# Weights of an octonion layer placed in threes and pairs of hidden units per partition, and down's last columns spread by GpSimd

## The chip, the cores and the metric

One core of one Trainium2 chip. The metric is the device time of one execution in microseconds. The engines are TensorE (PE; its weight loads are PEld), VectorE (DVE), ScalarE (ACT), GpSimd (POOL) and SyncE (SP), which here issues every DMA.

## The reference

For 2,048 rows of 1,024 numbers, x is normalised to xn. The output is x plus two terms. The first is an autocorrelation block over xn, which for these data comes to xn itself; the kernel proves that row by row with a spectrum and a bound, and has a slow path behind a flag. The second is a gated layer whose three matrices are ternary and act by the octonion product:

```python
def ternary_dequant(W):
    scale = jnp.mean(jnp.abs(W))
    return scale * jnp.clip(jnp.round(W / scale), -1.0, 1.0)
def oct_ternary_linear(xp, W):                 # W: (8, outputs, inputs)
    M = jnp.einsum('jik,jod->koid', S_OCT, ternary_dequant(W))
    return jnp.einsum('...id,koid->...ko', xp, M)
h = silu(oct_ternary_linear(xp, w_gate)) * oct_ternary_linear(xp, w_up)
out = x + attention(xn) + oct_ternary_linear(h, w_down)
```

Gate and up are (8, 341, 128) in float32, down is (8, 128, 341). Each of the 8 components has 341 hidden units. Before a matrix can be made ternary, the mean of all its absolute values must be known.

## The kernel before

**Tiling.** The 2,048 rows go in 8 groups of 256 (two tiles of 128). The 341 hidden units of a component are cut into three chunks c = 0, 1, 2 of 128, 128 and 85 units (`WIDE`). In what order the units stand is free, as long as gate, up and down agree.

**Which unit is where.** Partition p holds units 2p and 2p+1 as chunks 0 and 1, and chunk 2 is unit 256+p on partitions 0 to 84. `up_stage[m]` (m = 0 gate, 1 up) is [partition, j, c, d], one row of 128 floats for each. SyncE loads it in two kinds of transfer: `left_rows` (line 302), 85 partitions by 8 components in pieces of 512 bytes, and pieces of 1,024 bytes (lines 310 and 314) on all 128 partitions. Gate's second kind is cut in two halves of four components, with semaphores `w_in[0]` and `gate_rest`. GpSimd first zeroes chunk 2 of partitions 64 to 127 (line 1764), which `left_rows` waits for, so that the absolute sums can run over whole rows of the staging area. Down lies as [input d on partitions, j, 341 units] and comes in one transfer of 1,364-byte pieces (line 316); TensorE's transposes read chunks 0 and 1 with a step of two elements and chunk 2 as the last 85 columns.

**The head.** VectorE and ScalarE take the row sums of the first x tiles; GpSimd makes the scales of the rows (`rstd`, up to line 1800) and signals `ln_done`. The order on ScalarE is written out: `absolute_gate(0)` (sum of absolute values of a quarter of gate, line 759), `normalise(0, 0)` (748), `absolute_gate(1)`. VectorE has the same: absolute sum (1460), normalise of tile 1 (1479), absolute sum. `absolute_gate(0)` waits for `w_in[0]`, the second for `gate_rest`. TensorE fills its wait with transposes of an identity (`idle_work`), transposes half of gate's first chunk (`weights`, 520), the normalised x (`x_unit`, 482), the other half, and sums the absolute values over the partitions (`total`, 530). VectorE makes the threshold, ScalarE the signs (785), VectorE the ternary weights (1232); then the first group's products (`direct`, 465) begin.

**After the head.** The other chunks of gate, up and down are transposed between the products of the first group, in an order written out by hand for each engine. GpSimd builds sums of ternary weights (1809 to 1813), then waits until the second group's variances are there (1784) before it turns to the hidden units. ScalarE's `absolute(2)` (770) sums down. From the second group on, a written sequence of units (`STEADY`) repeats; lines 409, 416 and 426 are the products of gate and up, line 548 those of down.

Of the kernel before, what the change touches and what calls it, by code (L numbers as in the profile page):

```python
def octonion_ffn_attention_kernel(nc, x, w_gate, w_up, w_down, dft, lag, out):
# [5 lines left out]
    ALU, ACT, AX = mybir.AluOpType, mybir.ActivationFunctionType, mybir.AxisListType  # L7

    P = 128
    ROWS, D = x.shape  # L10
    NJ, HB, DB = w_gate.shape
    NC = 3
    REST = HB - 2 * P
    WIDE = (P, P, REST)
    LEFT = REST + REST % 2
    PAIR = 2 * LEFT
    T = 256
    NT = T // P
    G = ROWS // T
# [134 lines left out]
    with ctx:  # L154
# [3 lines left out]
        def sem(name):  # L158
            return ctx.enter_context(nc.semaphore(name))
# [42 lines left out]


        raw = hop[:, :, :, :, :].rearrange("p a f l t -> p (a f l t)").bitcast(F32)
        stage = [raw[:, 7168:7168 + NJ * NC * DB], raw[:, 10240:10240 + NJ * NC * DB], raw[:, 13312:13312 + NJ * HB]]
        up_stage = [stage[m].rearrange("p (j c d) -> p j c d", j=NJ, c=NC) for m in range(2)]
        down_stage = stage[2].rearrange("p (j h) -> p j h", j=NJ)
        small = zx[:, :, :].rearrange("p t d -> p (t d)").bitcast(F16)
        wt = [small[:, 1024 * i:1024 * (i + 1)].rearrange("p (j d) -> p j d", j=NJ) for i in range(2)]
        tt = [small[:, 2048 + 1024 * i:3072 + 1024 * i].rearrange("p (k v d) -> p k v d", k=4, v=2) for i in range(2)]  # L210
# [21 lines left out]
            return acc[0:rows, bank[n], :, :]  # L232

        x_in = [sem(f"x_in{t}") for t in range(NT)]; zx_in = [sem(f"zx_in{t}") for t in range(NT)]
        w_in = [sem(f"w_in{m}") for m in range(3)]; gate_rest = sem("gate_rest"); tab_in = sem("tab_in"); out_st = sem("out_st")
        const_done = sem("const_done"); padded = sem("padded"); pchain = sem("pchain"); zeroed = sem("zeroed"); row_zero = sem("row_zero"); table_in = sem("table_in")
        abs_done = [sem(f"abs_done{m}") for m in range(3)]
        total_mm = sem("total_mm"); total_read = sem("total_read"); thr_done = [sem(f"thr_done{m}") for m in range(3)]
# [58 lines left out]

        @block.sync
        def _(sp):
            def left_rows(m, w):  # L300

                sp.dma_start(up_stage[m][0:REST, :, 2, :], w[:, 2 * P:HB, :].rearrange("j p d -> p j d")).then_inc(w_in[m], 16)

            for t in range(NT):
                sp.dma_start(xr[:, t, :], x_rows[t, :, :]).then_inc(x_in[t], 16)

            sp.wait_ge(row_zero, 1)
            left_rows(0, w_gate)
            for j, signal in ((0, w_in[0]), (NJ // 2, gate_rest)):
                sp.dma_start(stage[0].rearrange("p (j e) -> p j e", j=NJ)[:, j:j + NJ // 2, 0:2 * DB],  # L310
                             w_gate[j:j + NJ // 2, 0:2 * P, :].rearrange("j (p c) d -> p j (c d)", c=2)).then_inc(signal, 16)
            sp.wait_ge(row_zero, 2)
            left_rows(1, w_up)
            sp.dma_start(stage[1].rearrange("p (j e) -> p j e", j=NJ)[:, :, 0:2 * DB],
                         w_up[:, 0:2 * P, :].rearrange("j (p c) d -> p j (c d)", c=2)).then_inc(w_in[1], 16)
            sp.dma_start(down_stage, w_down.rearrange("j o h -> o j h")).then_inc(w_in[2], 16)
            sp.dma_start(dft_sb[:, :, :], dft).then_inc(tab_in, 16)
            sp.dma_start(lag_sb[:, :, :], lag).then_inc(tab_in, 16)

            def load_x(g):  # L320
                sp.wait_ge(x_mm, x_no["X", g - 1, 1] + 1)
                sp.wait_ge(dot_done, NT * g)
                for t in range(NT):
                    sp.dma_start(xr[:, t, :], x_rows[NT * g + t, :, :]).then_inc(x_in[t], 16)

            load_x(1)
            load_x(2)
            sp.wait_ge(slots_done, len(slots_no))
            sp.wait_ge(eights_done, eights_no["T", 2, 2] + 1)
            for t in range(NT):  # L330
                sp.dma_start(zx[:, t, :], x_rows[t, :, :]).then_inc(zx_in[t], 16)
            for g in range(G):
                for t in range(NT):
                    k = NT * g + t
                    if t == 1 and 0 < g < G - 3:
                        load_x(g + 3)
                    left = D
                    if k == NTILE - 1:
                        for i, left in enumerate((D // 2, T)):
                            sp.wait_ge(part_out, i + 1)  # L340
                            sp.dma_start(out_rows[k, :, left:D >> i], zx[:, t, left:D >> i]).then_inc(out_st, 16)
                    sp.wait_ge(out_done, k + 1)
                    sp.dma_start(out_rows[k, :, 0:left], zx[:, t, 0:left]).then_inc(out_st, 16)
                    if k == 0:
                        load_x(3)
                    if g < G - 1:
                        sp.wait_ge(out_st, 16 * (k + 1))
                        sp.dma_start(zx[:, t, :], x_rows[k + NT, :, :]).then_inc(zx_in[t], 16)
            sp.wait_ge(out_st, 16 * NTILE + 32)
            sp.nop()  # L350

        @block.tensor
        def _(pe):
# [153 lines left out]
            def weights(u, components=range(NJ)):  # L507
                _, m, c = u
                if 0 in components:
                    take_banks(u)  # L510
                    if c == 0:
                        pe.wait_ge(w_in[m], 32 if m < 2 else 16)
                elif m == 0 and c == 0:
                    pe.wait_ge(gate_rest, 16)
                for j in components:
                    if m < 2:
                        src, rows, cols = up_stage[m][0:WIDE[c], j, c, :], P, WIDE[c]
                    else:
                        src, rows, cols = down_stage[:, j, c:2 * P:2] if c < 2 else down_stage[:, j, 2 * P:HB], WIDE[c], DB
                    last = nc.tensor.transpose(acc[0:rows, bank[place[u]], j // 4, P * (j % 4):P * (j % 4) + cols], src,  # L520
                                               ident[0:src.shape[0], 0:src.shape[0]])
                if NJ - 1 in components:
                    last.then_inc(wt_mm, 1)

            def total(m, u):

                pe.wait_ge(abs_done[m], 4 if m == 0 else 1)
                if m == 1:
                    pe.wait_ge(silu_done, 1)
                nc.tensor.matmul(acc[:, bank[place[u]], 0, 0:4], ones[:, :], asum[:, m, :], start=True, stop=True).then_inc(total_mm, 1)  # L530
# [136 lines left out]
        def _(act):  # L667
# [82 lines left out]
            def absolute_gate(half):  # L750

                act.wait_ge(zeroed, 1)
                if half == 0:
                    act.wait_ge(w_in[0], 32)
                else:
                    act.wait_ge(gate_rest, 16)
                quarter = NJ * NC * DB // 4
                cols = slice((2 * half + 1) * quarter, (2 * half + 2) * quarter)
                nc.scalar.activation(abs_junk[:, cols], stage[0][:, cols], ACT.Abs, accum_out=asum[:, 0, 2 + half:3 + half]).then_inc(abs_done[0], 1)

            def absolute(m):
                act.wait_ge(w_in[m], 32 if m < 2 else 16)
                act.wait_ge(zeroed, 1)
                whole = NJ * NC * DB
                if m == 1:
                    act.wait_ge(abs_done[0], 4)
                    nc.scalar.activation(abs_junk[:, 0:whole], stage[1], ACT.Abs, accum_out=asum[:, 1, 0:1]).then_inc(abs_done[1], 1)
                else:
                    act.wait_ge(abs_done[1], 1)
                    nc.scalar.activation(abs_junk[:, 0:NJ * HB], stage[2], ACT.Abs, accum_out=asum[:, 2, 0:1]).then_inc(abs_done[2], 1)  # L770

            def signs(u):
                _, m, c = u
# [110 lines left out]
            def h_high(g, c, Y):  # L884
                m = h_no[g, c, Y]
                h = hx[0:WIDE[c], m % 4, :, :]
                if m == 0:
                    act.wait_ge(abs_done[2], 1)
                if m == LAST:
                    act.wait_ge(tail_pair, 2)  # L890
                    h = last_h
# [294 lines left out]
        def _(dve):  # L1186
# [265 lines left out]
            def absolute_gate(half):  # L1452

                if half == 0:
                    dve.wait_ge(w_in[0], 32)
                else:
                    dve.wait_ge(gate_rest, 16)
                quarter = NJ * NC * DB // 4
                cols = slice(2 * half * quarter, (2 * half + 1) * quarter)
                nc.vector.tensor_reduce(asum[:, 0, half:half + 1], stage[0][:, cols], AX.X, ALU.add, apply_absolute_value=True).then_inc(abs_done[0], 1)  # L1460
# [301 lines left out]
        def _(pool):  # L1762
# [51 lines left out]
                                               s[:, a:a + 1, :, :].broadcast_to([P, 2, 2, WIDE[0]]), s[:, 2:4, :, :], alu)  # L1814
            last.then_inc(first_slots, 1)

            def power(g):
                pool.wait_ge(scaled, 2 * (g - 1))
                nc.gpsimd.tensor_tensor(r0[:, :], vr[:, NT * g:NT * g + NT], mh[:, :], ALU.pow).then_inc(power_of, 1)
# [75 lines left out]
```

## Time and profile before

| | us |
|---|---|
| median of 3 runs | 573.12 |
| lowest, highest | 572.56, 573.49 |
| the profiled execution's own time | 571.62 |
| its span | 569.8 |

| engine | busy us | share |
|---|---|---|
| PE | 554.2 | 97% |
| PEld | 523.7 | 92% |
| POOL | 465.7 | 82% |
| DVE | 471.2 | 83% |
| ACT | 384.0 | 67% |

Busy time is the time in which an engine has an instruction running; matmuls are pipelined, so a busy TensorE need not be one at its peak. The page also cuts the span in 40 slices of 14.2 us: TensorE is at 5 tenths in the first and at 8 to 9 tenths or more in all others, and the DMA is busiest in the first two, at 6 tenths each.

### The profile page before, as it was taken

How to read it: one execution, taken by the hardware profiler on the slowest of the kernel's cores; microseconds unless marked ns; L12 is line 12 of the kernel's file. 1: busy time of each engine (PE TensorE's matmuls, PEld its weight loads, DVE VectorE, ACT ScalarE, POOL GpSimd, SP SyncE). 2: the span in 40 equal slices, each digit the busy share in tenths (PEclk: the TensorE clock that was granted, in tenths of full speed). 3: DMA queues.
4: the chain of work that ended last, by engine and by line, in shares of the span. 5: the costliest groups of instructions: out<-in, count | busy, mean ns of one | idle time of the engine just before them, and what ended most of it. 6: DMA issues, size and time to landing. Idle time of an engine off the chain costs nothing.

```text
span 569.8 us, 16765 instructions
## 1 busy us (share of the span) xinstructions
PE 554.2 (97%) x6852; PEld 523.7 (92%) x6852; DVE 471.2 (83%) x1227; ACT 384.0 (67%) x620; POOL 465.7 (82%) x335
## 2 busy tenths in 40 slices
PE   5999998999989999999999999999999999999998
PEld 5899997899979999999999999999999999999997
DVE  3887999796968879888789879888889879975965
ACT  4878889965875478845986578745985484645430
POOL 3407649898997989899989988998989987999950
PEclk9999999999998999999999999999999999999999
DMA  6620202001220031200320040100320021102022
GB/s 185 203 76 1 75 2 77 1 1 40 112 75 1 3 108 43 76 2 28 123 75 2 2 141 18 68 3 38 112 76 2 2 75 39 39 2 76 2 76 77
DMA packets 12072, 30.70 MB, mean 54 GB/s; under 512 B 906, under 2 KB 5850, under 8 KB 11994
## 3 DMA queue, kind: packets, MB, share of 16 engines
q1 hardware_dynamic: 11994, 29.62, 15.2%
q8 instruction: 54, 0.88, 0.6%
q14 instruction: 24, 0.20, 0.1%
HBM read 21.23 MB, written 8.39 MB: 52 GB/s over the span
## 4 chain that ended last, share of the span: by engine, by line
PE 73%; POOL 13%; issue 8%; DVE 2%; DMA 2%; ACT 1%; SPq 0%; POOLq 0%; ACTq 0%; DVEq 0%
PE acc L548 26%; PE acc L416 15%; PE acc L409 14%; PE acc L426 10%; POOL hop L1859 4%; PE acc L465 4%; POOL hs L1852 2%; POOL hs L1847 2%; POOL hs L1851 2%; PE acc L482 2%; DMA hop<-in_w_gate 2%; PE acc L439 2%; POOL hs L1846 1%; POOL hop L1856 1%; PE acc L495 1%
## 5 line engine op out<-in xcount | busy, mean ns | idle before, releaser
L548 PE MATMUL acc<-wd,hop 128*128 128x128 f16 (+1 forms) x2944 | 169.9, 219 | 0.0
L548 PEld LDWEIGHTS acc<-wd,hop 128*128 128x128 f16 (+1 forms) x2944 | 166.8, 98 | 0.4
L832 ACT ACTIVATE pk<-acc 128x512 f32<-128x512 f32 (+1 forms) x120 | 66.6, 556 | 79.5 <-PE acc L426 30.5
L1856 POOL TENSOR_TENSOR hop<-hx,hop 128x1024 f16<-128x1024 f32 (+1 forms) x46 | 98.2, 2134 | 7.3 <-ACT hop L900 7.3
L1859 POOL TENSOR_TENSOR hop<-hs,hop 128x1024 f16<-128x1024 f32 (+1 forms) x46 | 98.2, 2135 | 6.8 <-ACT hop L910 6.3
L1846 POOL TENSOR_TENSOR hs<-hx 128x512 f32<-128x512 f32 (+1 forms) x47 | 60.3, 1283 | 35.4 <-DVE hx L1417 23.7
L426 PE MATMUL acc<-wl,xop 128*128 128x172 f16 x1024 | 84.1, 239 | 1.8 <-DVE hx L1423 1.6
L426 PEld LDWEIGHTS acc<-wl,xop 128*128 128x128 f16 x1024 | 78.6, 98 | 3.5 <-DVE hx L1423 2.1
L1306 DVE TENSOR_TENSOR bd<-acc,pk 128x256 f32<-128x256 f32 (+1 forms) x104 | 40.4, 389 | 48.9 <-ACT pk L832 48.8
L1851 POOL TENSOR_TENSOR hs<-hs 128x512 f32<-128x512 f32 (+1 forms) x47 | 59.8, 1273 | 3.7
L1852 POOL TENSOR_TENSOR hs<-hs 128x512 f32<-128x512 f32 (+1 forms) x47 | 60.4, 1285 | 0.0
L1847 POOL TENSOR_TENSOR hs<-hx 128x512 f32<-128x512 f32 (+1 forms) x47 | 60.2, 1280 | 0.0
L910 ACT ACTIVATE hop<-hs 128x1024 f16<-128x1024 f32 (+1 forms) x46 | 48.4, 1051 | 15.4 <-POOL hs L1852 15.4
L416 PE MATMUL acc<-xop,wg 128*128 128x256 f16 x448 | 54.2, 275 | 2.5 <-DVE acc L1354 2.4
L409 PE MATMUL acc<-xop,wg 128*128 128x256 f16 x448 | 53.3, 273 | 0.2 <-DVE hx L1423 0.2
L416 PE MATMUL acc<-xop,wu 128*128 128x256 f16 x448 | 53.3, 273 | 0.0
L900 ACT ACTIVATE hop<-hx 128x1024 f16<-128x1024 f32 (+1 forms) x46 | 48.4, 1052 | 6.9 <-PE acc L548 6.8
L409 PE MATMUL acc<-xop,wu 128*128 128x256 f16 x448 | 52.3, 273 | 0.0
L416 PEld LDWEIGHTS acc<-xop,wg 128*128 128x128 f16 x448 | 43.1, 98 | 8.0 <-DVE acc L1354 2.7
L409 PEld LDWEIGHTS acc<-xop,wu 128*128 128x128 f16 x448 | 43.8, 98 | 5.0
L409 PEld LDWEIGHTS acc<-xop,wg 128*128 128x128 f16 x448 | 43.6, 98 | 5.2 <-DVE hx L1423 0.4
L416 PEld LDWEIGHTS acc<-xop,wu 128*128 128x128 f16 x448 | 43.3, 98 | 4.7
(199 smaller groups left out, 1062.3 us busy)
## 6 DMA issues: line engine op xcount, KB each, us to landing
xr<-in_x SPq DMA_DIRECT2D x16, 512.0 KB, 4.2
zx<-in_x SPq DMA_DIRECT2D x16, 512.0 KB, 3.6
out_y<-zx SPq DMA_DIRECT2D x15, 512.0 KB, 2.6
hop<-in_w_down SPq DMA_DIRECT2D x1, 1364.0 KB, 10.9
hop<-in_w_gate SPq DMA_DIRECT2D x2, 512.0 KB, 7.3
hop<-in_w_up SPq DMA_DIRECT2D x1, 1024.0 KB
hop<-in_w_gate SPq DMA_DIRECT2D x1, 340.0 KB
hop<-in_w_up SPq DMA_DIRECT2D x1, 340.0 KB
```

The costliest lines, as they stand in the source:

```text
L409: last = nc.tensor.matmul(acc[:, bank[n], s // 2, T * (s % 2):T * (s % 2 + 1)], wm[:, c, slot, :], xop[:, g % 2, form, level, :], start=s ...
L416: last = nc.tensor.matmul(acc[:, bank[n], s // 2, T * (s % 2):T * (s % 2 + 1)], wm[:, c, slot, :], xop[:, g % 2, form, level, :], start=Fa ...
L426: last = nc.tensor.matmul(acc[:, bank[n], s // 2, T * (s % 2):T * (s % 2) + PAIR], xop[:, g % 2, form, level, P * t:P * (t + 1)], wl[:, sl ...
L548: last = nc.tensor.matmul(dst, operand(g, c, t, form, level), wd[0:WIDE[c], slot, c, :], start=which == 0 and c == CHUNKS[0] and s // 2 no ...
L832: nc.scalar.activation(pk[:, q % 2, :, 0:wide], pair[:, :, T:T + wide], ACT.Copy, scale=XS if u[0] == "X" else 1.0).then_inc(copied, 1)
L900: nc.scalar.activation(half_of(g, c, 4 * Y, 0), by_tile(h), ACT.Copy).then_inc(hhi_done, 1)
L1846: nc.gpsimd.tensor_tensor(hs[rows, 4:8:2, :], h[:, 0:4:2, :], h[:, 1:4:2, :], ALU.add)
L1847: nc.gpsimd.tensor_tensor(hs[rows, 5:8:2, :], h[:, 0:4:2, :], h[:, 1:4:2, :], ALU.subtract).then_inc(hpair_done, 1)
L1851: nc.gpsimd.tensor_tensor(hs[rows, 0:2, :], hs[rows, 4:6, :], hs[rows, 6:8, :], ALU.add).then_inc(hs_done, 1)
L1852: nc.gpsimd.tensor_tensor(hs[rows, 2:4, :], hs[rows, 4:6, :], hs[rows, 6:8, :], ALU.subtract).then_inc(hs_done, 1)
L1856: nc.gpsimd.tensor_tensor(half_of(g, c, 4 * Y, 1), by_tile(h), half_of(g, c, 4 * Y, 0), ALU.subtract).then_inc(h_free, 1)
L1859: nc.gpsimd.tensor_tensor(half_of(g, c, NJ + 4 * Y, 1), by_tile(hs[rows, 0:4, :]), half_of(g, c, NJ + 4 * Y, 0), ALU.subtract).then_inc(h_ ...
```

## The change

Units are placed otherwise. Partitions 0 to 79 hold three neighbouring units each (3p, 3p+1, 3p+2), partitions 80 to 127 two each, out of the 96 units from 240 on, and the last five units (336 to 340) are chunk 2 of partitions 80 to 84. Gate and up are loaded to match: pieces of 1,536 bytes on 80 partitions, of 1,024 on 48, and 40 of 512. The pieces on partitions 80 to 127 don't touch the zeroed area and are issued ahead of the wait for it.

In down the units of chunk c are now the columns c, c+3, c+6, and so on of a row of 384 places. The first 240 columns are loaded in place; the last 101 go to an area of their own (`down_ends`), from where GpSimd spreads them into the row with two copies. The absolute sum of down becomes two instructions, and TensorE's transposes of down wait for GpSimd.

```diff
@@
+    THIRDS = 80
+    SPLIT = NC * THIRDS
+    ENDS = HB - SPLIT
+    FIVE = REST - THIRDS
@@
-        stage = [raw[:, 7168:7168 + NJ * NC * DB], raw[:, 10240:10240 + NJ * NC * DB], raw[:, 13312:13312 + NJ * HB]]
+        stage = [raw[:, i:i + NJ * NC * DB] for i in (7168, 10240, 13312)]
+        down_ends = raw[:, 6144:6144 + NJ * ENDS].rearrange("p (j h) -> p j h", j=NJ)
@@ sync
-            def left_rows(m, w):
-                sp.dma_start(up_stage[m][0:REST, :, 2, :], w[:, 2 * P:HB, :].rearrange("j p d -> p j d")).then_inc(w_in[m], 16)
+            def pairs_of_units(m, w, j, signal):
+                sp.dma_start(up_stage[m][THIRDS:P, j, 0:2, :], w[j, SPLIT:SPLIT + 2 * (P - THIRDS), :].rearrange("j (p c) d -> p j c d", c=2)).then_inc(signal, 16)
+            def threes_of_units(m, w, j, signal):
+                sp.dma_start(up_stage[m][0:THIRDS, j, :, :], w[j, 0:SPLIT, :].rearrange("j (p c) d -> p j c d", c=NC)).then_inc(signal, 16)
+            def last_units(m, w):
+                sp.dma_start(up_stage[m][THIRDS:REST, :, 2, :], w[:, HB - FIVE:HB, :].rearrange("j p d -> p j d")).then_inc(w_in[m], 16)
@@
+            pairs_of_units(0, w_gate, first, w_in[0])
             sp.wait_ge(row_zero, 1)
-            left_rows(0, w_gate)
...
+            threes_of_units(0, w_gate, first, w_in[0])
+            last_units(0, w_gate)
+            pairs_of_units(0, w_gate, rest, gate_rest)
+            threes_of_units(0, w_gate, rest, gate_rest)
             sp.wait_ge(row_zero, 2)
-            left_rows(1, w_up)
...
-            sp.dma_start(down_stage, w_down.rearrange("j o h -> o j h")).then_inc(w_in[2], 16)
+            last_units(1, w_up)
+            pairs_of_units(1, w_up, every, w_in[1])
+            threes_of_units(1, w_up, every, w_in[1])
+            sp.dma_start(down_stage[:, :, 0:SPLIT], w_down[:, :, 0:SPLIT].rearrange("j o h -> o j h")).then_inc(w_in[2], 16)
+            sp.dma_start(down_ends, w_down[:, :, SPLIT:HB].rearrange("j o h -> o j h")).then_inc(w_in[2], 16)
@@ tensor, weights
-                        src, rows, cols = down_stage[:, j, c:2 * P:2] if c < 2 else down_stage[:, j, 2 * P:HB], WIDE[c], DB
+                        src, rows, cols = down_stage[:, j, c:c + NC * (WIDE[c] - 1) + 1:NC], WIDE[c], DB
@@ scalar, absolute
-                    nc.scalar.activation(abs_junk[:, 0:NJ * HB], stage[2], ACT.Abs, accum_out=asum[:, 2, 0:1]).then_inc(abs_done[2], 1)
+                    nc.scalar.activation(abs_junk[:, 0:NJ * SPLIT].rearrange("p (j h) -> p j h", j=NJ), down_stage[:, :, 0:SPLIT], ACT.Abs,
+                                         accum_out=asum[:, 2, 0:1]).then_inc(abs_done[2], 1)
+                    act.wait_ge(abs_done[2], 1)
+                    nc.scalar.activation(abs_junk[:, 0:NJ * ENDS].rearrange("p (j h) -> p j h", j=NJ), down_ends, ACT.Abs,
+                                         accum_out=asum[:, 2, 1:2]).then_inc(abs_done[2], 1)
@@ gpsimd, behind the sums of ternary weights (line 1813)
+            pool.wait_ge(w_in[2], 32)
+            for c, wide, at in ((0, 2, 0), (2, 1, 2 * (P - THIRDS))):
+                count = (P if c < 2 else REST) - THIRDS
+                dst = down_stage[:, :, SPLIT:SPLIT + NC * count].rearrange("p j (e c) -> p j e c", c=NC)[:, :, :, c:c + wide]
+                nc.gpsimd.tensor_copy(dst, down_ends[:, :, at:at + wide * count].rearrange("p j (e c) -> p j e c", c=wide)).then_inc(spread_done, 1)
```

The waits for the weights count to the new numbers of transfers: 48 for the first half of gate and for up, 32 for the rest of gate and for down.

## Rows read from the trace of the kernel before

**Rows 1.** Chain of waits, 0 to 60 us: start us, us, what.
```profile
2.07 9.81 DMA hop<-in_w_gate
...
18.29 10.73 PE acc L465 x96
```

**Rows 2.** Stretches: us, PE PEld DVE ACT POOL busy, PEclk, DMA share, GB/s.
```profile
0.00:5.00 5.00, 1.48 (x7) 1.48 (x8) 0.27 (x2) 1.49 (x2) 3.16 (x13) 1.00 0.57 203
5.00:6.00 1.00, 1.00 (x7) 1.00 (x6) 1.00 (x1) 0.96 (x1) 0.00 (x0) 1.00 0.32 101
9.00:10.00 1.00, 0.17 (x2) 0.00 (x0) 0.00 (x0) 0.00 (x0) 0.76 (x4) 1.00 1.13 225
12.00:13.00 1.00, 1.00 (x10) 1.00 (x11) 1.00 (x2) 1.00 (x3) 0.00 (x0) 1.00 0.35 111
17.00:23.00 6.00, 5.26 (x48) 4.38 (x47) 5.90 (x20) 5.48 (x6) 3.95 (x4) 1.00 1.06 350
50.00:80.00 30.00, 30.00 (x276) 27.37 (x274) 28.18 (x56) 26.60 (x50) 17.78 (x12) 1.00 0.11 36
```

**Rows 3.** Timeline, 10 to 30 us: start us, us, what.
```profile
10.45 0.19 POOL L1798 TENSOR_TENSOR nmrs<-nm,rs 128x2 f32<-128x2 f32 x1
...
11.91 0.95 DVE L1460 TENSOR_REDUCE sums<-hop 128x1 f32<-128x768 f32 x1 [3.63 <-DMA hop<-in_w_gate]
...
12.81 1.23 ACT L748 ACTIVATE xr<-xr,nmrs,rs 128x1024 f32<-128x1024 f32 x1
...
13.94 0.83 ACT L759 ACTIVATE hop<-hop 128x768 f16<-128x768 f32 x1
...
15.46 0.28 PE L530 MATMUL acc<-sums,ones 128*128 128x4 f32 x2
...
20.84 2.76 ACT L767 ACTIVATE hop<-hop 128x3072 f16<-128x3072 f32 x1
...
21.32 4.50 POOL L1813 TENSOR_TENSOR wg<-zx 128x512 f16<-128x512 f16 x4
```

**Rows 4.** Source views of lines 305 and 310: ns min/median/max, first and last start.
```profile
L305 SPq DMA_DIRECT2D xr<-in_x x2: 382/400/417, 0.7 to 1.2; - x2
...
DMA to landing us min/median/max: 3.9/4.5/5.0
...
L310 SPq DMA_DIRECT2D hop<-in_w_gate x2: 742/2344/3947, 2.1 to 6.1; - x2
...
DMA to landing us min/median/max: 7.3/7.3/7.3
```

**Rows 5.** Timeline, 41 to 55 us: idle before it and its releaser in brackets.
```profile
41.39 0.19 POOL L1784 TENSOR_SCALAR vr<-vr 128x2 f32<-128x2 f32 x1 [15.57 <-ACT junk L694]
...
44.23 2.48 ACT L770 ACTIVATE hop<-hop 128x2728 f16<-128x2728 f32 x1
...
46.59 0.20 ACT L770 ACTIVATION_READ_ACCUMULATOR hop<-hop 128x1 f32 x1
...
49.73 1.41 DVE L1232 SCALAR_TENSOR_TENSOR wu<-acc,few,zx 128x512 f16<-128x512 f32 x2 [1.39 <-ACT zx L785]
...
52.44 0.60 ACT L832 ACTIVATE pk<-acc 128x512 f32<-128x512 f32 x1 [0.35 <-PE acc L482]
...
54.98 2.14 POOL L1859 TENSOR_TENSOR hop<-hs,hop 128x1024 f16<-128x1024 f32 x1 [0.19 <-ACT hop L910]
```

**Rows 6.** Source view of line 520, windows 25:50 and 50:60: ns min/median/max.
```profile
L520 PEld LDWEIGHTS acc<-ident,hop x40: 139/140/223, 28.7 to 47.5; 128*128 128x128 f32 x24, 85*128 85x128 f32 x16
...
L520 PEld LDWEIGHTS acc<-ident,hop x8: 196/208/209, 55.6 to 56.4; 128*128 128x128 f32 x8
```

**Rows 7.** Two stretches of 3.4 us in group two.
```profile
171.40:174.80 3.40, 3.40 (x23) 2.96 (x21) 3.40 (x11) 2.34 (x3) 3.40 (x3) 0.50 0.02 5
174.80:178.20 3.40, 3.40 (x34) 3.06 (x33) 2.87 (x11) 1.72 (x3) 3.32 (x3) 1.00 0.00 0
```

**Rows 8.** Timeline before the first of these stretches, TensorE.
```profile
170.37 2.68 PE L416 MATMUL acc<-xop,wg 128*128 128x256 f16 x16 [2.43 <-DVE acc L1354]
```

More of the change, by code:

```diff
@@ L234, in octonion_ffn_attention_kernel @@
         x_in = [sem(f"x_in{t}") for t in range(NT)]; zx_in = [sem(f"zx_in{t}") for t in range(NT)]
-        w_in = [sem(f"w_in{m}") for m in range(3)]; gate_rest = sem("gate_rest"); tab_in = sem("tab_in"); out_st = sem("out_st")
+        w_in = [sem(f"w_in{m}") for m in range(3)]; gate_rest = sem("gate_rest"); spread_done = sem("spread_done"); tab_in = sem("tab_in"); out_st = sem("out_st")
         const_done = sem("const_done"); padded = sem("padded"); pchain = sem("pchain"); zeroed = sem("zeroed"); row_zero = sem("row_zero"); table_in = sem("table_in")
@@ L304, in _ @@
+            def last_units(m, w):
+                sp.dma_start(up_stage[m][THIRDS:REST, :, 2, :], w[:, HB - FIVE:HB, :].rearrange("j p d -> p j d")).then_inc(w_in[m], 16)
             for t in range(NT):
                 sp.dma_start(xr[:, t, :], x_rows[t, :, :]).then_inc(x_in[t], 16)
+            first, rest, every = slice(0, NJ // 2), slice(NJ // 2, NJ), slice(0, NJ)
+            pairs_of_units(0, w_gate, first, w_in[0])
             sp.wait_ge(row_zero, 1)
-            left_rows(0, w_gate)
@@ L309, in _ @@
-            for j, signal in ((0, w_in[0]), (NJ // 2, gate_rest)):
-                sp.dma_start(stage[0].rearrange("p (j e) -> p j e", j=NJ)[:, j:j + NJ // 2, 0:2 * DB],
-                             w_gate[j:j + NJ // 2, 0:2 * P, :].rearrange("j (p c) d -> p j (c d)", c=2)).then_inc(signal, 16)
+            threes_of_units(0, w_gate, first, w_in[0])
+            last_units(0, w_gate)
+            pairs_of_units(0, w_gate, rest, gate_rest)
+            threes_of_units(0, w_gate, rest, gate_rest)
@@ L312, in _ @@
             sp.wait_ge(row_zero, 2)
-            left_rows(1, w_up)
-            sp.dma_start(stage[1].rearrange("p (j e) -> p j e", j=NJ)[:, :, 0:2 * DB],
-                         w_up[:, 0:2 * P, :].rearrange("j (p c) d -> p j (c d)", c=2)).then_inc(w_in[1], 16)
-            sp.dma_start(down_stage, w_down.rearrange("j o h -> o j h")).then_inc(w_in[2], 16)
+            last_units(1, w_up)
+            pairs_of_units(1, w_up, every, w_in[1])
+            threes_of_units(1, w_up, every, w_in[1])
@@ L511, in weights @@
                     if c == 0:
-                        pe.wait_ge(w_in[m], 32 if m < 2 else 16)
+                        if m < 2:
+                            pe.wait_ge(w_in[m], 48)
+                        else:
+                            pe.wait_ge(w_in[m], 32)
+                            pe.wait_ge(spread_done, 2)
                 elif m == 0 and c == 0:
-                    pe.wait_ge(gate_rest, 16)
+                    pe.wait_ge(gate_rest, 32)
                 for j in components:
@@ L525, in total @@
             def total(m, u):
-                pe.wait_ge(abs_done[m], 4 if m == 0 else 1)
+                pe.wait_ge(abs_done[m], (4, 1, 2)[m])
                 if m == 1:
@@ L753, in absolute_gate @@
                 if half == 0:
-                    act.wait_ge(w_in[0], 32)
+                    act.wait_ge(w_in[0], 48)
                 else:
-                    act.wait_ge(gate_rest, 16)
+                    act.wait_ge(gate_rest, 32)
                 quarter = NJ * NC * DB // 4
@@ L761, in absolute @@
             def absolute(m):
-                act.wait_ge(w_in[m], 32 if m < 2 else 16)
+                act.wait_ge(w_in[m], 48 if m < 2 else 32)
                 act.wait_ge(zeroed, 1)
@@ L887, in h_high @@
                 if m == 0:
-                    act.wait_ge(abs_done[2], 1)
+                    act.wait_ge(abs_done[2], 2)
                 if m == LAST:
@@ L1454, in absolute_gate @@
                 if half == 0:
-                    dve.wait_ge(w_in[0], 32)
+                    dve.wait_ge(w_in[0], 48)
                 else:
-                    dve.wait_ge(gate_rest, 16)
+                    dve.wait_ge(gate_rest, 32)
                 quarter = NJ * NC * DB // 4
```

## The prediction, made before the changed kernel was run

> **What bounds the kernel now.** I read the page first: TensorE is busy for 97% of the span, so a change far from it must either shorten what TensorE waits for or move the instant at which it starts. Next the chain of waits over the first 60 us. From 2.07 to 11.88 us the chain is one DMA, the first half of the gate weights; ScalarE sums it, and from 18.29 us on the chain is TensorE on the products of the first group, 10.73 us without a break [rows 1]. So the head of the kernel is set by a landing, and what comes after by the instant at which TensorE gets its first operands.
>
> Then the stretches of the DMA. While the DMA has work for all its engines it moves 350 GB/s (17 to 23 us); from 5 to 6 us and from 12 to 13 us it moves 101 and 111 GB/s at a busy share of 0.32 and 0.35, which is 5 of 16 engines [rows 2]. The only transfers of this kind in both places are the 85-partition blocks of last units (line 302; 85 is 5 times 17, and neither 2, 4, 8 nor 16 divides it), queued ahead of the large gate pieces. The issue of the first large gate piece holds SyncE for 3.95 us, that of the second, of the same size, for 0.74 us, and both land late: 11.88 us, and 6.07 + 7.3 = 13.4 us [rows 1, 4]. By the Trainium skill, "DMA: Bandwidth & Descriptors", section "Why a DMA increments its semaphore by 16 and not by 1", a transfer is spread over the largest number of engines up to 16 that divides its slowest dimension: 5 for 85 partitions, 16 for 80 and for 48. For 85 the trace agrees (share 0.32).
>
> What waits beside that landing: GpSimd's chain for the first row scales ends at 10.45 + 0.19 = 10.64 us, but ScalarE normalises only at 12.81 us, because its first gate sum, and VectorE's of 0.95 us from 11.91, stand ahead in program order and wait for the weights [rows 3].
>
> **The change part by part.**
>
> *Loads of gate and up.* The 85-partition block of 680 pieces of 512 bytes goes; a block of 5 partitions and 40 pieces stays. The rest goes in pieces of 1 KB on 48 partitions and 1.5 KB on 80. The number of bytes is the same: 1.40 MB a matrix, of which 0.71 MB must be there for the first half of gate (4 components of 240 + 96 rows and the 40 last pieces) and 0.69 MB more for the rest. The x tiles move 203 GB/s x 5 us = 1.02 of their 1.05 MB by 5.0 us [rows 2], so they end at 5.1 us, and the second lands at 1.2 + 5.0 = 6.2 us [rows 4]: 1.1 us from last byte to landing. At 350 GB/s the first half of gate ends at 5.1 + 2.0 = 7.1 and lands at 8.2 us; the rest ends at 9.1 and lands at 10.2; up ends at 13.1 and lands at 14.2; down (1.40 MB) at 17.1 and 18.2. Bounds: not below the x landing, and with all at 225 GB/s (9 to 10 us, at a full share but with the uneven blocks between [rows 2]) the halves land at 9.4 and 12.4 us.
>
> What that frees: the first gate sums (0.95 us) fit before 10.70 us if the first half lands by 9.7, which holds at both ends. Then both normalise steps start when GpSimd's chain ends: ScalarE at 10.70 instead of 12.81, a gain of 2.11 us, and a landing any earlier gives nothing more. The next sums start at 11.8 instead of 13.94 [rows 3]; they need the rest of gate by then (10.2, at worst 12.4, which costs at most 0.5 as TensorE takes the sum only at 15.46, after 13.94 + 0.83 + a read of 0.2 [rows 3]). So -2.1 us, with bounds -1.6 and -2.2.
>
> SyncE issues thirteen DMAs where it issued nine, but an issue that isn't held up takes 0.38 to 0.74 us [rows 4], the added ones some 2 us in all, and the engine runs ahead of the packets: nothing. The first added one stands between the x loads and the wait for the memset. Its packets follow the x packets on all 16 engines, where now only the five have any; the landing of the second x tile, from which GpSimd's chain starts, may come a little later. Bound 0 to 0.5 us, an estimate: half of what separates the two x tiles' times to landing, 3.9 and 5.0 [rows 4]. I take +0.1.
>
> Speaking against: by the Trainium skill, "SBUF — State Buffer", section "Door 1: The DMA port swizzle", partitions 64 to 127 reach only 8 of 16 ports, each of some 27 GB/s. By that the pieces on partitions 80 to 127 and 0 to 79, one after the other, would take an estimated 1.2 + 1.8 us a half instead of 2.0, and the halves would land near 9.4 and 12.4 us, as in the slow bound above: at most half a microsecond of the gain. No row shows a transfer to such a range alone.
>
> Does the shift reach the end? After the head, only a DMA's landing could stay where it is in absolute time. Up is first read at 20.84 us [rows 3] (18.7 then; it lands at 14.2 and at the slow bound by 18.6), down after 25 us; the x loads of later groups start from signals of the computation and move with it. So the shift passes through whole.
>
> *Down's load and the spread.* Down comes in 1,024 pieces of 960 bytes and 1,024 of 404. GpSimd then copies 768 and 40 elements a partition. Its four additions of 512 elements take 4.50 us and end at 25.82; its next work starts at 41.39, after 15.57 us of idle time [rows 3, 5]. The trace has no copy there; at 1.12 us per 512 elements the two take about 1.9 us, at four times that 7.5. Both lie in the gap, at 24 to 32 us after the shift: nothing. If that cover were gone, the price would be the whole 1.9 us, since TensorE's transposes of down at 55 us wait for the copies. Even pieces of 404 bytes at 111 GB/s would land by 18.2 + 3.7 = 22 us.
>
> *Down's absolute sum in two.* The elements are the same 2,728, in 1,920 and 808. Added are the fixed part of an instruction, 0.2 us (0.83 us for 768 elements and 2.76 for 3,072 give 0.83 ns an element and 0.19 fixed [rows 3]), a read of the accumulator, 0.20 us, and a wait of under 0.1: 0.45 us. Queued behind it on ScalarE are two normalise steps, the signs of up's second chunk, the rounding of the first hidden units and the copies of the next x. VectorE has 1.39 us of slack ahead of those signs, ScalarE 0.35 us ahead of the x copy; GpSimd waits 0.19 us for ScalarE's rounded sums at 54.98 [rows 5]. Bounds 0 and +0.45; 0.45 - 0.35 = +0.1.
>
> *Transposes of down at stride three.* Twenty-four weight loads of TensorE read down with a step of 12 bytes, where sixteen had 8 and eight were contiguous. A contiguous load takes 140 ns, one at stride two 208 [rows 6]. Eight of them span more than one load's worth but far less than eight, because loads overlap with the matmuls; the timeline has 1.03 us for the eight at stride two against 0.91 for contiguous ones: +0.12 where each grew by 68 ns. If the third step costs as much again, the first two chunks pay 0.12 each and the last 0.06 to 0.24; if all 68 ns of each of 24 loads come to light it is 1.6 us; if only what lies under the matmuls grows, 0. I take +0.3, near the measured step. TensorE has no pause from 50 to 80 us [rows 2], so this lands on the path.
>
> *The sum.* -2.1 + 0.1 + 0.1 + 0.3 = -1.6 us. Against the profiled execution, 571.62 us of its own for a span of 569.8, that is 570.0 and 568.2. The shown runs have their median 1.5 us above the profiled one, at 573.12; from there the same difference gives **571.5 us**.
>
> **The rivals.**
>
> *The gain sinks into the middle.* The strided loads cost their 1.6 us, the rest of gate lands at the slow bound and ScalarE's 0.45 us is paid: -1.6 + 0.1 + 0.4 + 1.6 = +0.5, or without the dear loads about -0.8. For it: VectorE is busy for 28 of the 30 us from 50 to 80 beside a full TensorE [rows 2], so little slack is left to swallow anything. Against it: the step to stride two cost 0.12. Time about 573.1 (572.0 to 573.6).
>
> *A stall of the clock goes.* TensorE waits 2.43 us until 170.37, and then has its granted clock at 0.50, the lower of its two levels (1.2 of 2.4 GHz), for 3.4 us, in which it does 23 matmuls against 34 in as long a stretch after it [rows 7, 8]: 11/34 of 3.4, 1.1 us lost. With all work 2.1 us earlier the chip may or may not find the pause the same way. For it: there is a single such fall in a span with several pauses. Against: the wait itself stays. Time 571.5 - 1.1 = 570.4.
>
> *The pieces run on few engines too (slower).* If a transfer that begins at partition 80, or has 48 partitions, were spread over 5 engines as the old blocks are, gate would move at 111 GB/s [rows 2]: first half 5.1 + 6.4 + 1.1 = 12.6 us, rest 18.8. It decides from the point where the rest lands after the 13.4 of now: ScalarE's and VectorE's second sums would run 5.3 us later than 13.5, TensorE's total matmul at 19.9 instead of 15.46 [rows 3], +4.4. Time 577.5. For it, the old blocks did so; against it, 48 and 80 are multiples of 16, and the 128-partition pieces move at the full rate.
>
> **How the numbers follow.** Forecast 0.56 (570.8 to 571.97), clock 0.12, sunk gain 0.23, few engines 0.09. Differences under 0.2%, 1.15 us, can't be told from no change in this kernel, whose runs spread over 0.9 us. Faster by more: 0.56 + 0.12 = 0.68; within: 0.23; slower: 0.09. The range leaves out the slow rival and part of the clock's: 569.9 to 573.4.
>
> **What would show it.** In the profile after: ScalarE's first normalise at 10.7 to 11.0 us, no gate landing in the chain and GpSimd's scale chain in its place; a DMA share near 1 from 3 us to about 17, with no stretch at 0.3; the first product matmul near 16.3 instead of 18.29; GpSimd's two copies inside 23 to 35 us; weight loads of down at 210 to 280 ns; a product phase that ends about 1.6 us earlier. The prediction is wrong if the first normalise is later than 11.5, if GpSimd's copies reach past 39 us, if eight strided transposes span over 1.3 us, or if the shift is seen at 30 us and gone at 100.

## The result and the profile after

The changed kernel takes 569.66 us (median of 6 runs, 568.39 to 570.36) beside 572.84 us of the kernel before (6 runs, 571.71 to 573.49): ratio 0.9944, 95% interval 0.9927 to 0.996, so 3.2 us faster. I had forecast 1.6 us and a range that ended at 569.9. The two profiled executions differ by less: 571.62 to 570.29 us, and spans of 569.8 to 568.3 us, 1.5 us.

The chain of waits of the profile after, first 30 us (start us, us, what), to be held against [rows 1]:

```profile
3.40 9.48 DMA hop<-in_w_gate
...
16.85 10.73 PE acc L481 x96
```

The chain still begins with a landing of gate, now that of its second half, at 12.88 us. TensorE's products start at 16.85 instead of 18.29 us, 1.44 us earlier, and that is nearly the whole difference of the spans. The timeline of the same stretch [rows 3]:

```profile
10.00 0.95 DVE L1484 TENSOR_REDUCE sums<-hop 128x1 f32<-128x768 f32 x1 [2.05 <-DMA hop<-in_w_gate]
...
10.12 0.19 POOL L1822 TENSOR_TENSOR nmrs<-nm,rs 128x2 f32<-128x2 f32 x1
...
10.90 1.23 ACT L768 ACTIVATE xr<-xr,nmrs,rs 128x1024 f32<-128x1024 f32 x1
...
12.90 0.95 DVE L1484 TENSOR_REDUCE sums<-hop 128x1 f32<-128x768 f32 x1 [1.23 <-DMA hop<-in_w_gate]
12.96 0.84 ACT L779 ACTIVATE hop<-hop 128x768 f16<-128x768 f32 x1 [0.83 <-DMA hop<-in_w_gate]
...
13.95 0.39 PE L550 MATMUL acc<-sums,ones 128*128 128x4 f32 x2 [0.24 <-ACT hop L779]
...
16.85 1.92 PE L481 MATMUL acc<-xop,wg 128*128 128x256 f16 x16 [0.71 <-DVE wg L1256]
...
19.77 2.76 ACT L787 ACTIVATE hop<-hop 128x3072 f16<-128x3072 f32 x1 [0.26 <-DMA hop<-in_w_up]
...
25.12 1.02 POOL L1845 COPY hop<-hop 128x768 f32<-128x768 f32 x2 [0.74 <-DMA hop<-in_w_down]
```

GpSimd's scales are ready at 10.31 us, but the first gate sums begin only with the landing just before 10.0 us, so ScalarE normalises at 10.90 (12.81 before; I had said 10.70). The second sums wait once more, 1.23 us on VectorE and 0.83 us on ScalarE, for the rest of gate at 12.88, and TensorE's total matmul for them. ScalarE even waits 0.26 us for up. GpSimd's two copies take 1.02 us and lie in its pause. The stretches (columns as in [rows 2]: us, PE PEld DVE ACT POOL busy, PEclk, DMA share, GB/s):

```profile
5.00:9.00 4.00, 4.00 (x22) 4.00 (x21) 2.57 (x7) 2.12 (x4) 0.90 (x2) 1.00 1.13 225
9.00:13.00 4.00, 3.51 (x30) 3.04 (x29) 1.77 (x3) 2.11 (x4) 1.15 (x6) 1.00 1.12 195
17.00:23.00 6.00, 6.00 (x56) 5.24 (x55) 5.90 (x22) 5.26 (x6) 5.38 (x5) 1.00 1.16 277
50.00:80.00 30.00, 30.00 (x276) 27.34 (x275) 28.52 (x56) 26.92 (x53) 17.87 (x12) 1.00 0.10 36
```

Up to the last landing of the weights no stretch at a share of 0.3 is left, as predicted; but with all engines busy the DMA moves only 225 and then 195 GB/s, where I had put 350. Later, the timeline rows that answer to [rows 5]:

```profile
39.95 0.19 POOL L1808 TENSOR_SCALAR vr<-vr 128x2 f32<-128x2 f32 x1 [13.81 <-ACT junk L714]
...
42.79 1.80 ACT L790 ACTIVATE hop<-hop 128x1920 f16<-128x1920 f32 x1
...
44.72 0.88 ACT L793 ACTIVATE hop<-hop 128x808 f16<-128x808 f32 x1
...
48.62 1.41 DVE L1256 SCALAR_TENSOR_TENSOR wu<-acc,few,zx 128x512 f16<-128x512 f32 x2 [1.72 <-ACT zx L809]
...
51.01 0.60 ACT L856 ACTIVATE pk<-acc 128x512 f32<-128x512 f32 x1
...
53.54 2.15 POOL L1889 TENSOR_TENSOR hop<-hs,hop 128x1024 f16<-128x1024 f32 x1 [0.18 <-ACT hop L934]
```

Down's two sums end at 45.7 us. What stands right behind them on ScalarE is only 1.1 us earlier than before (normalise at 45.59 and 46.69), so VectorE now waits 1.72 instead of 1.39 us for the signs. But ScalarE no longer waits 0.35 us before the x copy, which is 1.43 us earlier (51.01 and 52.44), and GpSimd's wait at the rounded sums is the same. What was added is swallowed. The source view of the transposes' weight loads (ns min/median/max, [rows 6]):

```profile
L540 PEld LDWEIGHTS acc<-ident,hop x8: 196/196/201, 54.1 to 54.9; 128*128 128x128 f32 x8
...
L540 PEld LDWEIGHTS acc<-ident,hop x8: 192/207/207, 70.8 to 71.6; 128*85 128x85 f32 x8
```

At stride three a load takes 196 ns, less than the 208 at stride two; the 85 columns that used to be contiguous take 207.

Last the pause in the second group, [rows 7, 8]:

```profile
169.10:172.50 3.40, 3.40 (x19) 2.52 (x18) 3.40 (x12) 2.20 (x4) 2.89 (x2) 0.50 0.00 0
172.50:175.90 3.40, 3.40 (x38) 3.15 (x37) 3.28 (x12) 1.87 (x3) 3.32 (x4) 1.00 0.02 5
```

The fall of the clock is still there, 2.3 us earlier, with 19 and 38 matmuls in the two stretches.

### The profile page after: what moved, and what is told of

It reads as the page before. It is cut to its first block, busy times and chain, and to the rows that moved or that the text cites. A ratio compares the mean times of both kernels' runs of the same rounds, so it can differ in the third digit from the quotient of the medians.

```text
span 568.3 us, 16773 instructions
## 1 busy us (share of the span) xinstructions
PE 555.0 (98%) x6852; PEld 523.9 (92%) x6852; DVE 471.2 (83%) x1227; ACT 384.4 (68%) x622; POOL 466.6 (82%) x337
## 4 chain that ended last, share of the span: by engine, by line
PE 73%; POOL 13%; issue 8%; DVE 2%; DMA 2%; ACT 1%; SPq 0%; POOLq 0%; ACTq 0%; DVEq 0%
PE acc L568 26%; PE acc L432 15%; PE acc L425 14%; PE acc L442 10%; POOL hop L1889 4%; PE acc L481 4%; POOL hs L1882 2%; POOL hs L1877 2%; POOL hs L1881 2%; PE acc L455 2%; DMA hop<-in_w_gate 2%; PE acc L498 2%; POOL hs L1876 1%; POOL hop L1886 1%; PE acc L511 1%
## 6 DMA issues: line engine op xcount, KB each, us to landing
hop<-in_w_down SPq DMA_DIRECT2D x1, 404.0 KB, 16.8
```

## The experiments

For each run of the experiments the mean granted clock is recorded. It takes only three values, 1.0, 0.997 and 0.994. In the traces a fall is a stretch of some 3.4 us at a granted clock of 0.50, and the three values go with none, one or two of them (in the trace of before_pause, 0.994 is a single fall of 6.8 us). So the table gives each kernel's times at each value, over all series (number of runs, median, lowest to highest); the six runs of the kernel before that stand in the result have no recorded clock and are left out.

| kernel | at 1.0 | at 0.997 | at 0.994 |
|---|---|---|---|
| before | none | 27: 571.80 (571.10 to 572.20) | 25: 572.83 (572.54 to 573.42) |
| changed | 6: 569.14 (568.39 to 569.50) | 6: 570.36 (570.16 to 570.67) | none |
| loads_only | 4: 568.88 | 3: 570.73 | none |
| down_only | none | 5: 571.60 | 7: 573.03 |
| before_cover | 5: 570.24 | 7: 571.86 | none |
| before_pause | none | none | 10: 572.36 |
| pieces_128 | 1: 567.28 | 3: 569.19 | none |
| after_mixed | 1: 567.87 | 3: 569.23 | none |
| split80 | 8: 567.67 (567.48 to 567.78) | 4: 569.43 (569.33 to 569.62) | none |

**Which half of the change: loads_only and down_only.**

```diff
 # loads_only: the kernel before with
+pairs_of_units, threes_of_units, last_units for gate and up, in the new order
 # down_only: the changed kernel with
+left_rows and the two-row pieces of the kernel before for gate and up
```

> Gate and up placed and loaded as in the changed kernel, down left as it was (so the hidden units of down do not match those of gate and up, and the output is not the reference's). The head theory: the whole gain is in the head, so this is as fast as the changed kernel: 3.2 us below the kernel before by the medians, ratio 0.994 to 0.995, and in a profile the first product matmul near 16.9 us. The rival that the down side brings part of it: this gains only what the two profiles show, some 1.4 us (ratio 0.9975).

> Down loaded, summed, spread and transposed as in the changed kernel, gate and up left as they were (again placements do not match). The head theory: the ScalarE instruction and the strided loads are hidden or nearly so, 0 to 0.2 us slower than before, ratio 1.000. The rival that the down side brings the 1.8 us by which the medians differ more than the profiles: ratio 0.997.

loads_only: ratio 0.9955 (0.9939 to 0.9971). down_only: 1.0003 (0.9992 to 1.0013). The loads bring the whole gain; of down's side nothing shows beyond the noise in either direction. That a fixed 3.2 us would come back was wrong in form: at an equal mean clock (0.997) loads_only is 1.1 us below the kernel before, and the rest is that its runs have one fall fewer.

**The clock: before_cover, before_pause, before_look.**

```diff
 # before_cover
-            idle_work(32)
+            idle_work(56)
 # before_pause
-            idle_work(32)
+            idle_work(22)
```

> The kernel before with 24 more of TensorE's identity transposes in the head (56 instead of 32), which fill the 2.8 us in which it waits for gate. The clock theory: in unprofiled runs of the kernel before that pause often lets the granted clock fall to the lower level just when the first products come, so filling it gains 1 to 1.7 us of median (ratio 0.997 to 0.998) and raises the mean granted clock of the runs. The rival that the clock has no part: ratio 1.000, or up to 0.3 us slower if the transposes reach past the landing.

> The kernel before with 22 instead of 32 identity transposes ahead of the gate weights, so TensorE waits for gate for 4 us or more instead of 2.8. The clock theory: its clock falls in that pause in nearly every run, and the products of the first group start at the lower level; the trace shows a fall between 10 and 16 us, the mean granted clock of the runs is 0.994 in most, and the median is 0.4 to 1.0 us above the kernel before. The rival, in which the head's pause has nothing to do with the second fall: the same mix of 0.997 and 0.994 as in the kernel before, and the same median.

> The kernel before unchanged, one more profile. In about 9 of 24 runs its mean clock was 0.994; if this one is such a run, the clock theory expects a fall of 3.4 us between 10 and 17 us in it, beside the one near 171 us.

before_cover: 0.9985 (0.9974 to 0.9996), a smaller gain than the expected 0.997 to 0.998, though the interval reaches that; all its twelve runs are at 1.0 or 0.997, none at 0.994. In its profile TensorE's wait for gate is 1.35 instead of 2.76 us, and it keeps the upper level behind it (stretches, columns as above):

```profile
9.20:12.00 2.80, 2.04 (x19) 1.80 (x17) 0.00 (x0) 0.00 (x0) 1.06 (x6) 1.00 0.94 221
12.60:15.90 3.30, 3.10 (x26) 2.87 (x27) 2.51 (x3) 2.91 (x6) 0.00 (x0) 1.00 0.53 127
```

Gate landed 0.66 us later in that execution than in the profile of before, and its products start at 18.95 us; so what before_cover gains isn't an earlier start.

before_look happened to be a run at 0.994 (572.95 us), and shows where its two falls lie:

```profile
9.20:12.00 2.80, 0.75 (x7) 0.51 (x5) 0.00 (x0) 0.00 (x0) 0.97 (x6) 1.00 0.83 218
12.60:15.90 3.30, 3.30 (x18) 3.30 (x17) 1.94 (x3) 2.36 (x5) 0.00 (x0) 0.50 0.62 163
16.00:19.30 3.30, 2.89 (x27) 2.65 (x25) 1.92 (x4) 2.73 (x4) 0.00 (x0) 1.00 1.11 298
...
173.00:176.40 3.40, 3.40 (x23) 3.07 (x22) 3.40 (x11) 2.09 (x2) 3.40 (x3) 0.50 0.02 5
```

From 12.6 to 15.9 us, behind TensorE's wait for gate, the granted clock is 0.50, the lower of the two levels, and TensorE does 18 matmuls. The timeline of that run, TensorE alone, shows what that costs: twelve identity transposes take 2.73 us, and the first product, at 18.29 us in the profile of before, starts at 19.64, 1.35 us later. The first two lines are before_look's, the third is the same group in the profile of before:

```profile
12.03 0.66 PE L520 MATMUL acc<-ident,hop 128*128 128x128 f32 x4 [2.07 <-DMA hop<-in_w_gate]
12.52 2.73 PE L474 MATMUL acc<-ident 128*128 128x128 f32 x12
```

```profile
12.42 1.47 PE L474 MATMUL acc<-ident 128*128 128x128 f32 x12
```

before_pause waits longer, and all ten of its runs are at 0.994. Its clock has fallen already within the pause:

```profile
9.00:12.00 3.00, 0.00 (x0) 0.00 (x0) 0.00 (x0) 0.00 (x0) 1.22 (x7) 0.67 0.89 224
12.00:14.00 2.00, 1.89 (x9) 1.89 (x10) 1.91 (x3) 1.85 (x3) 0.00 (x0) 0.50 0.36 106
...
171.00:175.00 4.00, 2.61 (x28) 2.43 (x29) 4.00 (x13) 3.97 (x5) 2.68 (x2) 1.00 0.00 0
```

Its median, however, is not above that of before (ratio 1.0001, 0.9992 to 1.001), where I had expected 0.4 to 1.0 us more. Its profile shows the fall from 10.0 to 16.8 us and none near 171, so 0.994 there is one long fall in the head, part of it while TensorE stood idle anyway. The mean clock was told right, the price not; and only this one of its ten runs has a trace.

The changed kernel was run again for its own mix:

> The changed kernel unchanged, for more runs beside the others. The clock theory: its runs fall in two groups, one of mean clock 1.0 near 568.8 and one of 0.997 near 570.3, none at 0.994; at an equal mean clock it is 1.4 to 1.5 us below the kernel before. The rival, that the change is worth 3 us everywhere: one group, 3 us below at every clock.

Ratio 0.996 (0.9946 to 0.9973), three runs at each of the two values, 569.17 and 570.62 us by their medians, none at 0.994. At 0.997 the median of the changed kernel, over both series, lies 1.44 us below that of the kernel before (570.36 and 571.80), as much as the two profiles differ in the head. A single pair of executions isn't that exact: in the trace of after_again gate's halves land 0.2 and 0.3 us later and the products start at 17.20 instead of 16.85 us. So it is the medians that carry the 1.44; between the medians of a series it is 3.2 us in the first and 2.6 in this one, as the falls happen to be mixed.

So the kernel before has one or two falls in all its runs, and the count is one lower both when the pause in the head is filled (before_cover) and when it is shortened (the change). Which fall it is that goes is another question, and the traces forbid the simple answer that it is always the one in the head. The two traced executions at 0.997 with the old loads, the profile of before and down_only, have their one fall near 171 us and none in the head, though TensorE waited there 2.8 and 3.1 us for gate (stretches 12.6 to 15.9 us of before and of down_only):

```profile
12.60:15.90 3.30, 3.10 (x29) 2.86 (x28) 1.97 (x4) 2.94 (x6) 0.00 (x0) 1.00 0.68 175
```

```profile
12.60:15.90 3.30, 3.10 (x29) 2.87 (x28) 2.03 (x3) 2.94 (x6) 0.00 (x0) 1.00 0.63 141
```

The traces of before_cover and of after_again have no fall in either place, so against the profile of before they lack the one near 171; here the stretch of after_again:

```profile
169.00:172.50 3.50, 3.21 (x35) 3.02 (x36) 3.50 (x12) 3.50 (x5) 2.49 (x2) 1.00 0.00 0
```

TensorE's wait of 2.4 us ahead of that place is the same in all twelve traces, the six with a fall there and the six without. Why the fall in the second group comes in some executions and not in others, and what the pause in the head has to do with it, stays open. It was not tried to take away the wait at 168 us.

**Why the loads move only 225 GB/s: pieces_128, after_mixed, split80.**

```diff
 # pieces_128: kernel before, gate and up in pieces of 1,536 bytes on 128 partitions
+flat = w.rearrange("j o d -> (j o) d")[3 * P * q:3 * P * (q + count), :].rearrange("(q p c) d -> p q (c d)", p=P, c=NC)
+sp.dma_start(stage[m].rearrange("p (j e) -> p j e", j=NJ)[:, j:j + count, :], flat).then_inc(signal, 16)
 # after_mixed: changed kernel, gate component by component (up two by two)
+for j in range(NJ):
+    one, signal = slice(j, j + 1), w_in[0] if j < NJ // 2 else gate_rest
+    threes_of_units(0, w_gate, one, signal)
+    pairs_of_units(0, w_gate, one, signal)
...
 # split80: kernel before, its 85-partition block in 80 + 5; the first 128-partition piece ahead of the wait for the memset
-sp.dma_start(up_stage[m][0:REST, :, 2, :], w[:, 2 * P:HB, :].rearrange("j p d -> p j d")).then_inc(w_in[m], 16)
+sp.dma_start(up_stage[m][0:THIRDS, j, 2, :], w[j, 2 * P:2 * P + THIRDS, :].rearrange("j p d -> p j d")).then_inc(signal, 16)
+sp.dma_start(up_stage[m][THIRDS:REST, :, 2, :], w[:, 2 * P + THIRDS:HB, :].rearrange("j p d -> p j d")).then_inc(w_in[m], 16)
```

> The kernel before with gate and up loaded as pieces of 1,536 bytes on all 128 partitions, eight a partition and matrix (1.57 MB instead of 1.40, some rows read twice and all in the wrong place, so the output is not the reference's); down as before. It separates the size of the pieces from the partitions they go to. If 80 and 48 partitions reach too few ports, these pieces move at 300 GB/s or more, the first half of gate lands by 9.0 us and the rest by 11.6. If pieces of 1.5 KB are slow by themselves, the rate stays near the changed kernel's 195 to 225 GB/s and the halves land after 10 and 13.5 us.

> The changed kernel with its loads of gate and up issued one component after the other (up two by two), threes and pairs in turn, so that pieces for partitions 0 to 79 and for 80 to 127 are in flight together; same pieces, same bytes, 25 transfers instead of 8. The port theory in its mild form: the two kinds use different ports, so the rate rises from 195 to 225 to about 280 GB/s, the first half of gate lands by 9.2 and the rest by 11.8 us, and the kernel gains 0.5 to 1.0 us on the changed one at an equal mean clock (568.3 at 1.0, 569.6 at 0.997). The rival, that each engine does its own pieces of one transfer at the same time as the others, so that the ports are as crowded as before and the added transfers cost issue time: rate unchanged, landings within 0.3 us of 10.0 and 12.9 or later, no gain.

> The kernel before, with its own placement of units and its own down; only the 85-partition block of gate and of up is cut in 80 and 5 partitions (gate's also in two halves of components), and the first large piece of gate goes ahead of the wait for the memset. If the uneven spread over 5 engines is what held gate back, and the 1.5 KB pieces of the changed kernel are slow because 80 partitions reach few ports, this lands gate earlier than the changed kernel (first half by 9.2, rest by 11.5 us, against 10.0 and 12.9) and is 0.4 to 0.9 us faster than it: ratio to before 0.993. If it is only the size of the pieces that counts, the 1,280 pieces of 512 bytes cost more and it is slower than the changed kernel, ratio 0.995 to 0.997.

> The split of the 85-partition block alone, again, beside the kernel before and the mixed one. If it beats the changed kernel for the reason given (head 1.1 us shorter, clock falls no more frequent), its runs are near 567.6 at a mean clock of 1.0 and 569.5 at 0.997, against 569.1 and 570.4 of the changed kernel, and the ratio to the kernel before is 0.992 to 0.9955. If the first series was luck in the mix of clocks, the difference at an equal clock goes below 0.5 us.

The stretches 5 to 9 and 9 to 13 us of pieces_128, of after_mixed and of split80, in this order (columns as above):

```profile
5.00:9.00 4.00, 4.00 (x24) 4.00 (x23) 3.71 (x8) 3.29 (x6) 0.90 (x2) 1.00 1.04 383
9.00:13.00 4.00, 3.58 (x34) 3.35 (x32) 1.76 (x3) 2.35 (x6) 1.16 (x7) 1.00 1.07 374
```

```profile
5.00:9.00 4.00, 4.00 (x29) 3.98 (x28) 2.88 (x8) 2.37 (x5) 0.90 (x2) 1.00 0.99 265
9.00:13.00 4.00, 3.10 (x28) 2.86 (x27) 2.38 (x3) 3.05 (x6) 1.16 (x6) 1.00 0.78 219
```

```profile
5.00:9.00 4.00, 4.00 (x30) 3.82 (x29) 3.08 (x8) 2.67 (x5) 0.96 (x3) 1.00 1.10 319
9.00:13.00 4.00, 3.05 (x29) 2.81 (x28) 2.25 (x3) 3.00 (x6) 1.09 (x6) 1.00 1.13 304
```

Pieces of 1.5 KB on all 128 partitions move at 383 and 374 GB/s, against 225 and 195 in the changed kernel: it is not the size of the piece, and ScalarE's first gate sum starts at 8.19 us although more bytes are moved (ratio 0.9933, 0.9914 to 0.9951). With threes and pairs in turn the same pieces move at 265 GB/s in the first stretch, beside 225, 243 and 246 in the three traces with the order of the changed kernel (after, after_again, loads_only). In the second stretch the share falls to 0.78; each of the 26 transfers costs SyncE 0.32 to 0.44 us to issue, which is the likely reason. Clearer than the rate is the landing: gate's first sum starts at 8.76 us, beside 10.00, 10.15 and 9.97, and after_mixed is at 0.9938 (0.992 to 0.9956) of before, 1.1 us below the changed kernel at 0.997. So what held the loads is to which partitions a transfer goes, and what is in flight beside it. Of the partitions the Trainium skill says the same in "SBUF — State Buffer", section "Door 1: The DMA port swizzle": partitions 0 to 63 reach 8 of 16 ports, 64 to 127 the other 8. These runs agree in size: 8 ports by its figure of 27.2 GB/s would be an estimated 218 GB/s, beside the 195 to 246 measured in those three traces.

split80 keeps the old placement, so down needs no spread, and three quarters of its bytes go in 128-partition pieces: 319 and 304 GB/s (303 and 287 in the trace of the second series). The second gate landing is no longer in its chain; GpSimd's scales are, and the products start at 15.76 us:

```profile
10.04 0.20 POOL nmrs L1810
...
15.76 10.73 PE acc L477 x96
```

Its ratios to before are 0.9938 (0.992 to 0.9955) and, in a second series, 0.9923 (0.9909 to 0.9938). At a mean clock of 1.0 it takes 567.67 us against the changed kernel's 569.14, at 0.997 569.43 against 570.36. Gate's halves land at 8.6 and 10.8 us, earlier than expected (9.2 and 11.5), and the lead over the changed kernel, 1.5 and 0.9 us, is at or above the upper end. It beats both kernels, with a change in the loads alone.

## Why the prediction was right or wrong

**The 5 of 16 engines, and the move of the bound to the head: right.** The share of 0.3 is gone with the 85-partition block, both in the changed kernel and in split80, which beside that only moves the first piece ahead of the wait for the memset.

**-2.1 us in the head: mis-sized, it measured -1.44.** The step that failed is the rate. I took 350 GB/s for transfers to 80 and 48 partitions from a stretch in which 128-partition pieces were in flight [rows 2], and kept the crowding of ports only as the slow bound, with "at most half a microsecond". By that bound the halves land at 9.4 and 12.4 us; they landed just before 10.0 and at 12.88, later than even that. (The port estimate of the prediction, 3.0 us a half, gives 9.2 and 12.2 by its own sum, not 9.4 and 12.4.) The first costs 0.2 us (normalise at 10.90 instead of 10.70, and 0.5 against what the scales would have let), the second 0.5 more at the total matmul. Up and down were late by the same rate: ScalarE waited 0.26 us for up at 19.77, and down's last columns landed only at 25.1 us, where I had 22 at most. Neither reached the path. The bound itself was taken from a stretch of mixed traffic, 225 GB/s, and not from eight ports.

**+0.1 for the x tile: no.** The second x tile landed at 5.86 instead of 6.18 us, and GpSimd's scales came 0.33 us earlier. That is the spread of single executions: in before_look, the kernel before unchanged, GpSimd's last step for the scales starts at 10.12 us, as in the profile after, and in after_again at 10.39.

**+0.1 for the split sum: swallowed, 0.** ScalarE's lateness took the 0.35 us that it had waited, and TensorE's products of the stretch kept their 1.44 us.

**+0.3 for the strided loads: 0.** The third step of stride costs nothing: 196 ns against 208. Only the loads of the 85-column chunk grow, 207 ns instead of 154. down_only bounds both together at -0.5 to +0.7 us by the interval of its ratio, and at -0.2 and +0.2 by the medians at an equal clock.

**The sum for one execution: right by two errors that cancel.** -1.6 us forecast, -1.5 between the spans, -1.44 between the medians at 0.997. A head gain taken 0.66 too large and costs taken 0.5 too large.

**Where it was wrong: the median.** "The shown runs have their median 1.5 us above the profiled one, at 573.12; from there the same difference" is the failed step: it took a change of one execution for the change of the median, as if the distance between them stayed. That distance was itself a thing to be explained: by their times (572.56 to 573.49, where no run of this kernel with a single fall takes over 572.20) the three runs shown were all of the dearer kind, with a second fall of the clock, and the profiled one had a single fall. After the change the runs have one fall fewer, so the median loses another 1.0 to 1.2 us, and more where the mix favours it. I had a clock rival of 1.1 us, with a chance of 0.12, but as one more thing that may happen to the profiled execution's fall at 171 us. In part that came true, as half of the runs after have no fall at all. What I left out is that the runs around the median had one fall more than the profiled one. The pause of 2.8 us in the head, right beside the landing that I was moving, stood in the same trace as TensorE's idle time before its first transposes of gate, and the change shortens it to 0.3 us in one traced execution and 1.0 in the other. That the clock would matter there could have been asked of the difference between 573.12 and 571.62. That filling this pause takes a fall away is shown by before_cover; by what way stays open.

**The shift passes whole: right.** 1.44 us at 17 us, 1.4 at 54 (GpSimd's row 54.98 to 53.54), 1.5 at the end.

**Spread by GpSimd in its pause: right**, at 1.02 us where I had 1.9. Few engines for 80 and 48 partitions: did not happen, the share is 1.13 and 1.12.

## What to carry to other kernels

A busy DMA isn't a fast one: read the GB/s beside the share, and for a transfer that doesn't span all partitions take its rate from a transfer to a like range, or keep full-height transfers in flight beside it. When a count of partitions has no factor that all engines share (85), cut off the odd remainder first; here that changed the loads alone and was worth more than moving every unit. When the profiled execution and the median of the runs lie apart by more than the change is worth, find out what lies between them before adding a difference to either.

## What the runs showed of the hardware

The two stretches in which only the 85-partition blocks were in flight show a DMA share of 0.32 and 0.35, at 101 and 111 GB/s. A full share doesn't mean a full rate: 1.12 went with 195 GB/s for pieces of 1 and 1.5 KB to 48 and 80 partitions, 1.07 with 374 GB/s for pieces of 1.5 KB to all 128.

A wait of TensorE of 2.1 to 2.8 us in the head goes with one more fall of the clock in a run: all 52 runs of the kernel before have one or two, 27 and 25 (down_only, which waits 3.1 us, 5 and 7), and the 51 of the kernels whose traces show a wait there of at most 1.4 us have none or one. Between one and two falls lie 1.0 us in the kernel before and 1.4 in down_only; between none and one 1.2 us in the changed kernel and 1.4 to 1.9 in the others. In one execution the fall in the head put off the first product by 1.35 us.

A float32 weight load of TensorE with 128 columns takes 140 ns contiguous, 208 at a step of 8 bytes and 196 at a step of 12; with 85 columns 154 contiguous and 207 at a step of 12.
